# A state-space scan in a four-block transformer kernel: three per-chunk multiplies by C become one wide instruction, one state later

## The chip, the cores and the metric

The kernel runs on one core of a Trainium2 chip. The metric is the device time of one execution in microseconds (us), lower is better. It is the median of three executions.

## The reference, cut to what matters

The reference computes four sublayers on an input of 4 x 512 tokens of width 512, each followed by a residual addition and a layer norm: a selective state-space model (SSM), a mixture of experts, an attention, and a quantised MLP. The change touches the SSM alone. For one sequence `b`, one channel `d` of 512 and one state `n` of 16:

```
dt    = softplus(x_proj[:16] @ dt_proj + bias)          # per token and channel
dA    = exp(dt * A[d, n])
dBx   = dt * B[t, n] * x
h[t]  = dA[t] * h[t-1] + dBx[t]                         # the scan over 512 tokens
y[t]  = sum over n of C[t, n] * h[t, n]   + D * x
```

## The kernel before, in words

**Tiling.** Channels lie on the 128 partitions, so 512 channels make four chunks (`KC` = 4, c = 0 to 3), and the tokens of one sequence (`NB` = 512) lie along the free dimension. There are four sequences (`BATCH`, called batches below, b) of 16 states (`STATE`), so 64 steps n = 16 b + m, m being the state within the batch. Each step has four scans, one for each chunk.

**The engines' parts in one step**, all in `ssm` (L132 to L689). ScalarE (ACT) makes `da` = exp(dt A) for one chunk at a time into a ring of two PSUM tiles (L424); it may write the tile for scan i only when scan i - 2 is done (L417). GpSimd (POOL) makes `dbx` for all four chunks in one wide multiply (`inputs`, L294) into a ring of two. It may begin `dbx` of step n once the last scan of step n - 2 is done (L293). VectorE (DVE) runs the four scans (L561). TensorE (PE) spreads the row C[., n] over all partitions with one matmul into the one PSUM tile `cbc` (`spread`, L632), and may do so only when the multiplies of the step before have read it. DVE multiplies a chunk of `h` by `cbc` (`weigh`, L510), into a ring of two tiles `hc` of one chunk each. PE adds the product into the PSUM tile `y` of that chunk with a multiplication by the identity (`gather`, L651). The last chunk (c = 3) is multiplied by POOL instead (`weigh_last`, L305, from a copy of C in SBUF that a DMA broadcast; its gather is L646), except in the states m = 5 and 6 of batches 0 to 2, where DVE does it too (`pooled`, L188), because POOL has other work for the next batch close by.

**The order.** Each engine has its queue, written out by hand, and semaphores tie them. On DVE, `weigh(n, c-1)` stands right behind scan c of step n (L563), so that it never waits for the scan in front of it. At a batch's first state (m = 0) DVE also reads the finished sums of the batch before (`sums`, L523): chunks 0 to 2 behind scans 1 to 3 of m = 0, and chunk 3 at m = 2. At m = 2 of batches 0 and 1 it splits the C rows of a later batch into two parts (`split_c`, L459 and L461).

**Work for later batches**, spread over the states of a batch. ACT has the pieces of the softplus (L433 to L445): at count j = 4 m + c = 15 it takes a logarithm (L397), with a table load before and one behind it. At j = 36, 40, 48, 52 it copies a finished dt chunk (`copy_dt`, L401). PE projects rows (`project_rows`, L589) and dt (`project_z`, L605) for batch b + 2, and adds up the parts of dt for batch b + 1 in the states of `SUMMED` (L146), each time with four full fp32 matmuls (L615 to L621). POOL multiplies the masked logarithm (L271) twice in m = 7 and twice in m = 8, and dt by x (`scaled_x`, L276) in m = 11, 12, 13 and 15. There `inputs` of the next step stands behind it on POOL's queue.

After the last step, DVE reads the sums of batch 3 (L575), and a block boundary lets the layer norm begin.

## Time and profile before

| | us |
|---|---|
| median of the runs before | 1925.83 (1924.51 to 1928.50, 3 runs) |
| the profiled execution's own time, given as its span | 1927.0 |
| DVE busy over the span | 1494.8 (78%) |
| PE busy | 1704.9 (88%) |
| POOL busy | 688.5 (36%) |
| the 256 scans (DVE, L561) | 304.6 |
| the 198 multiplies by C on DVE (L510) | 131.3 |
| the 63 wide multiplies on POOL (L294) | 285.5 |

Only the span is known of the profiled execution, and it stands for its time. The table's shares are over the whole program. The SSM is its first part, from the start to about 464 us, and what matters there is read from that stretch alone. Busy time counts an instruction from its start to its end; where an engine's instructions overlap a little at their ends, the distance from one start to the next is what an instruction costs its queue.

### The profile page before, as it was taken

What the parts mean: (1) busy time and instruction counts of PE and PEld (TensorE: products, weight loads), DVE (VectorE), ACT (ScalarE), POOL (GpSimd) and SP (SyncE); (2) the same over time, 40 slices, a digit from 0 to 9 for tenths busy, and PEclk for the clock granted to TensorE, in tenths of its full rate; (3) what the DMA queues carried; (4) which work ended last, traced back from release to release, by engine and by line L of the source; (5) the groups of instructions that cost most, each with busy time, mean ns of one, the idle gap of its engine ahead of it and who ended that gap; (6) DMA issues with size and microseconds to landing.
All of it is one profiled execution on the core that took longest, in us unless ns stands there. A gap on an engine that the chain in (4) does not pass through costs nothing. (4 is left out here: it accounts for less than half of the span.)

```text
span 1927.0 us, 24366 instructions
## 1 busy us (share of the span) xinstructions
PE 1704.9 (88%) x7730; PEld 1038.8 (54%) x7730; DVE 1494.8 (78%) x2746; ACT 826.9 (43%) x1384; POOL 688.5 (36%) x419
## 2 busy tenths in 40 slices
PE   7888979777999995997788888888989999999997
PEld 2232323223677774885233333334768778788786
DVE  7999999999866666731788898884876776776677
ACT  5657464443414554321367777776521111111112
POOL 5898989996065544201130000000031320330100
PEclk8999989999999997998699999999989999999999
DMA  5344342331059996744443333320010000000002
GB/s 146 102 123 129 96 134 87 100 86 54 7 190 389 415 413 228 265 187 173 114 118 93 94 94 93 88 77 3 1 66 1 34 34 1 33 33 1 1 1 88
DMA packets 110702, 211.63 MB, mean 110 GB/s; under 512 B 18907, under 2 KB 35675, under 8 KB 109681
## 3 DMA queue, kind: packets, MB, share of 16 engines
q1 hardware_dynamic: 105457, 193.30, 30.5%
q0 software_dynamic: 5120, 16.78, 2.6%
q8 instruction: 64, 1.05, 0.2%
q14 instruction: 61, 0.50, 0.1%
HBM read 144.95 MB, written 62.65 MB: 108 GB/s over the span
## 5 line engine op out<-in xcount | busy, mean ns | idle before, releaser
L2022 DVE TENSOR_REDUCE att_top<-att_first 128x1 f32<-128x512 f32 x512 | 332.1, 686 | 70.3 <-PE att_first L1902 62.9
L561 DVE TENSOR_TENSOR_SCAN ssm_h<-ssm_da,ssm_dbx 128x512 f32<-128x512 f32 x256 | 304.6, 1207 | 6.4 <-ACT ssm_da L424 6.1
L294 POOL TENSOR_TENSOR ssm_dbx<-ssm_u,ssm_bbc 128x2048 f32<-128x2048 f32 x63 | 285.5, 4533 | 34.0 <-DVE ssm_h L561 30.8
L1984 ACT ACTIVATE att_prob<-att_second 128x1024 f32<-128x1024 f32 x256 | 248.1, 1022 | 87.5 <-PE att_second L1922 82.3
L651 PE MATMUL ssm_y<-ssm_hc,all_ident 128*128 128x512 f32 x396 | 224.3, 651 | 68.7 <-DVE ssm_hc L510 63.1
L424 ACT ACTIVATE ssm_da<-ssm_dt,ssm_minus_a 128x512 f32<-128x512 f32 x256 | 176.8, 691 | 188.7 <-DVE ssm_h L561 188.5
L2412 ACT ACTIVATE ffn_silu<-ffn_pg 128x256 f32<-128x256 f32 x112 | 43.2, 386 | 406.5 <-PE ffn_pg L129 406.5
L2277 POOL TENSOR_TENSOR pairs_raw<-pairs_raw,pairs_scales 128x512 f32<-128x512 f32 x42 | 42.3, 1042 | 489.7 <-DMA pairs_raw<-in_w 489.7
L1902 PE MATMUL att_first<-att_ks,att_qs 48*128 48x512 f32 x512 | 133.4, 510 | 65.2 <-DVE att_top L2022 50.5
L127 PE MATMUL ffn_pg<-pairs_wh,last_XH 128*128 128x512 f32 x448 | 176.7, 394 | 1.7 <-PEq L2080 1.7
L128 PE MATMUL ffn_pg<-pairs_wl,last_XH 128*128 128x512 f32 x448 | 176.5, 394 | 0.0
L129 PE MATMUL ffn_pg<-pairs_wh,last_XL 128*128 128x512 f32 x448 | 175.6, 392 | 0.0
L651 PEld LDWEIGHTS ssm_y<-ssm_hc,all_ident 128*128 128x128 f32 x396 | 65.1, 197 | 178.0 <-DVE ssm_hc L510 122.3
L1902 PEld LDWEIGHTS att_first<-att_ks,att_qs 48*128 48x128 f32 x512 | 53.6, 191 | 193.9 <-DVE att_top L2022 133.6
L2445 DVE TENSOR_TENSOR ffn_h<-ffn_pg,ffn_silu 128x256 f32<-128x256 f32 x112 | 47.4, 423 | 128.0 <-ACT ffn_silu L2412 127.7
L1937 PE MATMUL att_out<-att_prob,att_v 128*32 128x512 f32 x1024 | 137.2, 608 | 0.1
L510 DVE TENSOR_TENSOR ssm_hc<-ssm_cbc,ssm_h 128x512 f32<-128x512 f32 x198 | 131.3, 663 | 3.2 <-DVE ssm_h L561 2.1
L2284 POOL TENSOR_SCALAR pairs_wh<-pairs_raw 128x512 fp32r<-128x512 f32 x42 | 24.9, 628 | 234.3 <-PE ffn_py L129 234.3
L127 PE MATMUL ffn_py<-pairs_wh,ffn_hh 128*128 128x512 f32 x224 | 98.4, 439 | 0.0
L127 PEld LDWEIGHTS ffn_pg<-pairs_wh,last_XH 128*128 128x128 f32 x448 | 84.8, 189 | 21.8 <-issue 2.1
L1922 PE MATMUL att_second<-att_qs,att_ks 56*128 56x512 f32 x512 | 92.3, 416 | 4.7 <-DMA att_qs<-att_rows 2.9
L129 PEld LDWEIGHTS ffn_pg<-pairs_wh,last_XL 128*128 128x128 f32 x448 | 84.7, 189 | 18.7
(335 smaller groups left out, 3570.2 us busy)
## 6 DMA issues: line engine op xcount, KB each, us to landing
all_X<-in_w SPq DMA_DIRECT2D x29, 769.0 KB, 10.2
ssm_bbc<-brow_dram SPq DMA_DIRECT2D x64, 256.0 KB, 4.1
ssm_cbs<-crow_dram SPq DMA_DIRECT2D x58, 256.0 KB, 3.5
att_qs<-qk_dram SPq DMA_DIRECT2D x192, 64.0 KB, 2.2
att_ks<-qk_dram SPq DMA_DIRECT2D x192, 64.0 KB, 2.2
sorted_x<-ssm_zero SPq DMA_DIRECT2D x47, 256.0 KB, 3.6
sorted_y<-exp_y SPq DMA_DIRECT2D x47, 256.0 KB, 10.5
mlps_raw<-in_w SPq DMA_DIRECT2D x14, 769.0 KB, 9.8
```

The costliest lines, as they stand in the source:

```text
L127: pe.matmul(out, lh, rh, start=first, stop=False)
L128: pe.matmul(out, lh, rl, start=False, stop=False)
L129: return pe.matmul(out, ll, rh, start=False, stop=last)
L294: nc.gpsimd.tensor_tensor(dbx[:, n % 2], u[:, n // STATE % 2], bbc[:, n % RING, :].unsqueeze(1).to_broadcast([P, KC, NB]), ALU.mult).then_ ...
L424: nc.scalar.activation(da[:, i % 2, :], dt[:, b % 2, c, :], ACT.Exp, scale=minus_a[:, c, n % STATE:n % STATE + 1]).then_inc(da_ready, 1)
L510: nc.vector.tensor_tensor(hc[:, k % 2, :], cbc[:], h[:, n % 2, c, :], ALU.mult).then_inc(hc_ready, 1)
L561: nc.vector.tensor_tensor_scan(h[:, n % 2, c, :], da[:, i % 2, :], dbx[:, n % 2, c, :], 0.0, ALU.mult, ALU.add).then_inc(h_ready, 1)
L651: pe.matmul(y[:, c, :], g.ident[:], hc[:, k % 2, :], start=(m == 0), stop=(m == STATE - 1)).then_inc(y_own, 1)
L1902: pe.matmul(p_first[first_place(m) % FIRSTS][:], qs[w % RING][at, pair, qt * P:(qt + 1) * P], ks[w % RING][at, pair, :], start=True, stop= ...
L1937: mm = pe.matmul(p_out[VPAD * j:VPAD * (j + 1), :], v[s % RING][:, kt, VPAD * j:VPAD * (j + 1)], prob[step % 2][:, j, :], start=(kt == 0), ...
L1984: nc.scalar.activation(prob[step % 2][:, js, :], p_second[second_place(step, pair) % 2][:], ACT.Exp, scale=DK ** -0.5).then_inc(exp_done, 1)
L2022: nc.vector.tensor_reduce(top[w % 2][:, qt, item:item + 1], p_first[first_place(m) % FIRSTS][:], AX.X, ALU.max).then_inc(max_done, 1)
```

## The change

DVE's multiplies by C move one step later and become wide. For step n - 1 one instruction multiplies chunks 0 to 2 (0 to 3 in the states in which POOL does not take the last chunk) by `cbc`, read again for each chunk. It stands behind scan 1 of step n (behind scan 0 in the last step). `hc` becomes a ring of two steps of four chunks, and its semaphores count steps. The last step is still multiplied chunk by chunk, one behind scan 2, one behind scan 3 and one after the scans. PE's gathers of a step follow its wide multiply, so they come behind `spread` of the next step. The dt sums move to the states 6, 7, 9 and 10, the row projection to the front of m = 0, and the dt projection from m = 2..5 to m = 1..4. On DVE `sums` of chunks 0 to 2 move from m = 0 to m = 1, and the first waits for all of the batch's gathers of DVE's chunks. `split_c` moves from behind scan 1 to behind scan 2 of m = 2.

```diff
-        SUMMED = (7, 8, 10, 11)
+        SUMMED = (6, 7, 9, 10)
...
-        hc = sb("hc", [P, 2, NB])
+        hc = sb("hc", [P, 2, KC, NB])
...
-        def by_dve(n):
-            return KC * n - by_pool(n)
+        def wide(n):
+
+            return LAST if pooled(n) else KC
+
+        def weighed(n, c):
+
+            return n + 1 if n + 1 < STEPS else n + c + 1
...
-            def weigh(n, c):
-                k = by_dve(n) + c
-                dve.wait_ge(h_ready, KC * n + c + 1)
+            def weigh(n, lo, hi):
+                dve.wait_ge(h_ready, KC * n + hi)
                 dve.wait_ge(c_ready, n + 1)
-                if k >= 2:
-
-                    dve.wait_ge(y_own, k - 1)
-                nc.vector.tensor_tensor(hc[:, k % 2, :], cbc[:], h[:, n % 2, c, :], ALU.mult).then_inc(hc_ready, 1)
+                if n >= 2:
+
+                    dve.wait_ge(y_own, n - 1)
+                nc.vector.tensor_tensor(hc[:, n % 2, lo:hi, :], cbc[:].unsqueeze(1).to_broadcast([P, hi - lo, NB]),
+                                        h[:, n % 2, lo:hi, :], ALU.mult).then_inc(hc_ready, 1)
 
             def sums(b, c):
                 if c < LAST:
 
-                    dve.wait_ge(y_own, by_dve(STATE * (b + 1) - 1) + c + 1)
+                    dve.wait_ge(y_own, STATE * (b + 1))
...
                         if c < LAST or not pooled(n - 2):
-                            dve.wait_ge(hc_ready, by_dve(n - 2) + c + 1)
+                            dve.wait_ge(hc_ready, n - 1)
...
-                    if c:
-                        weigh(n, c - 1)
-                    elif n and not pooled(n - 1):
-                        weigh(n - 1, LAST)
                     if n == 0 and c == 0:
                         split_c(1)
-                    if m == 2 and c == 1 and b + 2 < BATCH:
+                    if b and m == 1 and c < 2:
+                        sums(b - 1, c)
+                        if c:
+                            sums(b - 1, c + 1)
+                    if n and c == (1 if n + 1 < STEPS else 0):
+                        weigh(n - 1, 0, wide(n - 1))
+                    if n + 1 == STEPS and c >= 2:
+                        weigh(n, c - 2, c - 1)
+                    if m == 2 and c == 2 and b + 2 < BATCH:
                         split_c(b + 2)
-                    if b and m == 0 and c:
-                        sums(b - 1, c - 1)
                     if b and m == 2 and c == 0:
                         sums(b - 1, LAST)
+            weigh(STEPS - 1, LAST - 1, LAST)
...
-                    pe.wait_ge(hc_ready, by_dve(n))
+                    pe.wait_ge(hc_ready, n)
...
-                    k = by_dve(n) + c
-                    pe.wait_ge(hc_ready, k + 1)
-                    pe.matmul(y[:, c, :], g.ident[:], hc[:, k % 2, :], start=(m == 0),
-                              stop=(m == STATE - 1)).then_inc(y_own, 1)
+                    pe.wait_ge(hc_ready, weighed(n, c))
+                    mm = pe.matmul(y[:, c, :], g.ident[:], hc[:, n % 2, c, :], start=(m == 0), stop=(m == STATE - 1))
+                    if c == wide(n) - 1:
+                        mm.then_inc(y_own, 1)
...
-                for c in range(LAST):
-                    if c == LAST - 1 and pooled(n) and n + 1 < STEPS:
-                        spread(n + 1)
+                if m == 0 and b + 2 < BATCH:
+                    for c in range(KC):
+                        project_rows(b + 2, c)
+                if n + 1 < STEPS:
+                    spread(n + 1)
+                for c in range(wide(n)):
                     gather(n, c)
-                    if n >= 2 and c == 0 and pooled(n - 2):
-                        gather(n - 2, LAST)
-                    if b + 2 < BATCH:
-                        if m == 0:
-                            project_rows(b + 2, c)
-                        if m == 1 and c == 0:
-                            project_rows(b + 2, LAST)
-                        if 2 <= m < 2 + KC and c == 1:
-                            project_z(b + 2, m - 2)
+                    if n and c == 0 and pooled(n - 1):
+                        gather(n - 1, LAST)
+                    if b + 2 < BATCH and 1 <= m < 1 + KC and c == 1:
+                        project_z(b + 2, m - 1)
                     if b + 1 < BATCH and m in SUMMED and c == LAST - 2:
                         sum_dt_first(b + 1, SUMMED.index(m))
                     if b + 1 < BATCH and m in SUMMED and c == LAST - 1:
                         sum_dt_last(b + 1, SUMMED.index(m))
-                if not pooled(n):
-                    if n + 1 < STEPS:
-                        spread(n + 1)
-                    gather(n, LAST)
-            gather(STEPS - 2, LAST)
             gather(STEPS - 1, LAST)
```

## Rows read from the trace of the kernel before

**Rows 1.** The first line of the profile's page.

```profile
span 1927.0 us, 24366 instructions
```

**Rows 2.** Windows, batch 1: busy of PE, PEld, DVE, ACT, POOL; clock, DMA, GB/s.

```profile
145.00:258.00 113.00, 96.68 (x197) 34.68 (x197) 109.92 (x126) 66.45 (x100) 102.52 (x41) 0.96 0.36 112
```

**Rows 3.** Groups by line, all scans (32 to 461 us): busy, mean ns, idle before.

```profile
L294 POOL TENSOR_TENSOR ssm_dbx<-ssm_u,ssm_bbc 128x2048 f32<-128x2048 f32 x63 | 285.5, 4533 | 34.0 <-DVE ssm_h L561 30.8 <-PE ssm_y L646 2.9
...
L510 DVE TENSOR_TENSOR ssm_hc<-ssm_cbc,ssm_h 128x512 f32<-128x512 f32 x198 | 131.3, 663 | 3.2 <-DVE ssm_h L561 2.1 <-PE ssm_cbc L632 0.4
```

**Rows 4.** DVE's waits, all scans: total, times, longest in us.

```profile
DVE ssm_h L561 <- ACT ssm_da L424: 6.1, 3, 2.1
DVE ssm_hc L510 <- DVE ssm_h L561: 2.1, 3, 0.7
```

**Rows 5.** Timeline (start, duration, engine, line) of DVE, one state of batch 3.

```profile
391.05 2.32 DVE L561 TENSOR_TENSOR_SCAN ssm_h<-ssm_da,ssm_dbx 128x512 f32<-128x512 f32 x2
393.30 0.66 DVE L510 TENSOR_TENSOR ssm_hc<-ssm_cbc,ssm_h 128x512 f32<-128x512 f32 x1
393.88 1.21 DVE L561 TENSOR_TENSOR_SCAN ssm_h<-ssm_da,ssm_dbx 128x512 f32<-128x512 f32 x1
...
397.30 2.32 DVE L561 TENSOR_TENSOR_SCAN ssm_h<-ssm_da,ssm_dbx 128x512 f32<-128x512 f32 x2
```

**Rows 6.** Groups by line and form: two-tensor operations of DVE, of two widths.

```profile
L1423 DVE TENSOR_TENSOR mlps_wl<-all_X,mlps_wh 128x1024 fp32r<-128x1024 f32 x29 | 35.2, 1215 | 0.0
...
L496 DVE TENSOR_TENSOR ssm_u<-ssm_dt,all_sums 128x512 f32<-128x512 f32 x4 | 2.5, 681 | 0.0
```

**Rows 7.** Timeline of POOL and DVE, the scans' first steps.

```profile
36.11 9.03 POOL L294 TENSOR_TENSOR ssm_dbx<-ssm_u,ssm_bbc 128x2048 f32<-128x2048 f32 x2
...
40.72 2.34 DVE L561 TENSOR_TENSOR_SCAN ssm_h<-ssm_da,ssm_dbx 128x512 f32<-128x512 f32 x2
```

**Rows 8.** Timeline of POOL, batch 0, from state 11's dbx to batch 1's first.

```profile
102.37 4.52 POOL L294 TENSOR_TENSOR ssm_dbx<-ssm_u,ssm_bbc 128x2048 f32<-128x2048 f32 x1 [0.85 <-DVE ssm_h L561]
106.85 1.27 POOL L305 TENSOR_TENSOR ssm_hp<-ssm_cbs,ssm_h 128x512 f32<-128x512 f32 x1
108.07 1.27 POOL L276 TENSOR_TENSOR ssm_u<-ssm_dt,all_sums 128x512 f32<-128x512 f32 x1
109.30 4.54 POOL L294 TENSOR_TENSOR ssm_dbx<-ssm_u,ssm_bbc 128x2048 f32<-128x2048 f32 x1
...
136.00 4.52 POOL L294 TENSOR_TENSOR ssm_dbx<-ssm_u,ssm_bbc 128x2048 f32<-128x2048 f32 x1
```

**Rows 9.** Timeline of DVE: state 12's wait, and batch 1's first scans.

```profile
118.09 0.69 DVE L510 TENSOR_TENSOR ssm_hc<-ssm_cbc,ssm_h 128x512 f32<-128x512 f32 x1 [0.70 <-DVE ssm_h L561]
...
141.13 2.32 DVE L561 TENSOR_TENSOR_SCAN ssm_h<-ssm_da,ssm_dbx 128x512 f32<-128x512 f32 x2
```

**Rows 10.** Timeline of PE: two gathers and a spread back to back.

```profile
121.46 1.02 PE L646 MATMUL ssm_y<-ssm_hp,all_ident 128*128 128x512 f32 x2
122.32 1.02 PE L651 MATMUL ssm_y<-ssm_hc,all_ident 128*128 128x512 f32 x2
123.27 0.49 PE L632 MATMUL ssm_cbc<-ssm_c_parts,ssm_sel 64*128 64x512 f32 x1
```

**Rows 11.** Timeline of ACT and DVE around the logarithm, batch 1, state 3.

```profile
166.53 0.68 ACT L424 ACTIVATE ssm_da<-ssm_dt,ssm_minus_a 128x512 f32<-128x512 f32 x1
...
172.47 2.35 DVE L561 TENSOR_TENSOR_SCAN ssm_h<-ssm_da,ssm_dbx 128x512 f32<-128x512 f32 x2 [2.05 <-ACT ssm_da L424]
```

**Rows 12.** Timeline of DVE: the last scan and the last sum.

```profile
458.11 1.21 DVE L561 TENSOR_TENSOR_SCAN ssm_h<-ssm_da,ssm_dbx 128x512 f32<-128x512 f32 x1
...
462.84 0.75 DVE L523 SCALAR_TENSOR_TENSOR all_sums<-all_sums,ssm_d,ssm_y 128x512 f32<-128x512 f32 x1 [0.96 <-PE ssm_y L646]
```

**Rows 13.** Windows: a stretch of batch 3 with a lower granted clock.

```profile
444.00:448.00 4.00, 3.97 (x6) 1.70 (x6) 4.00 (x5) 1.50 (x3) 3.50 (x3) 0.58 0.00 0
```

**Rows 14.** Timeline of PE: the gather that begins that stretch.

```profile
444.03 2.08 PE L651 MATMUL ssm_y<-ssm_hc,all_ident 128*128 128x512 f32 x2 [1.27 <-DVE ssm_hc L510]
```

## The prediction

> **What bounds the kernel now.** I read the page's first line for the profiled execution's length [rows 1]: 1927.0 us, 1.2 above the median of 1925.83. The sum is made against 1927.0, and the difference from the median is taken off at the end. The change lies within the scans, so the next views are of that stretch alone. The windows of batch 1 show DVE busy for 109.9 of 113 us and POOL for 102.5 [rows 2]: DVE bounds the stage, with POOL close behind. The groups by line name POOL's big item, 63 multiplies of 4.53 us with only 34 us of idle time before them in 428 us, and DVE's 198 multiplies by C of 0.663 us [rows 3]. DVE waits three times for ACT, 2.05 us each, at the logarithm, and three times 0.7 us in front of a multiply [rows 4]. The timeline gives the price that counts, the distance between starts [rows 5]: a state lasts 397.30 - 391.05 = 6.25 us. Two scans take 2.25, so a scan costs 1.125, and a multiply costs 393.88 - 393.30 = 0.58, although each lasts 0.66: the next instruction starts before this one has ended.
>
> **The wide multiply.** No row has its form. By width, a two-tensor operation takes 681 ns for 512 columns and 1215 for 1024 [rows 6], which is 1.043 ns a column. Three chunks then cost 0.58 + 1024 x 0.001043 = 1.65 us instead of 3 x 0.58 = 1.74, and four cost 2.18 instead of 2.32. Bounds: the multiplies' full fixed part would give 0.663 - 0.534 = 0.129 us for each instruction saved, not 0.58 - 0.534 = 0.046; at the other end reading C again for each chunk could cost as much as it saves, and the state stays at 6.25. I take 0.046, since rows 5 are this very queue. A state of DVE is then 4 x 1.125 + 1.65 = 6.15.
>
> The page "VectorE: DVE Perf Modes" of the Trainium skill (section on the TRN2 errata) gives a PSUM-source instruction a fixed cost of 120 cycles at 0.96 GHz, paid between instructions. By it each saved instruction would bring 0.125 us, and the sum would be the first rival's. The start-to-start distance in rows 5 disagrees.
>
> **The sum, by stretches.** Phases: "E" is the end of scan 3 of a batch's state 9, where POOL's chain of [rows 8] begins.
>
> 1. Up to the first scan of step 1 nothing changes: that scan starts at 40.72, just when POOL's first wide `dbx` is there (36.11 + 4.5 = 40.6) [rows 7]. The three multiplies of step 0 that lay in this wait leave it and have to be done later.
>
> 2. Batch 0, from there to E. Before, 28 multiplies: three for each of states 1 to 8, the extra ones of states 5 and 6, two of state 9: 16.24 us. After, the wide ones of states 0 to 8, 7 x 1.65 + 2 x 2.18 = 15.9. Gain 0.35, and 0.4 of a wait for PE in [rows 3] goes. At the logarithm ACT needs 172.47 - 166.53 = 5.94 us from its start behind scan 13 to scan 16 [rows 11], on either kernel. DVE covers it with 3 x 0.58 + 2 x 1.125 = 3.99 before and 1.65 + 2.25 = 3.90 after. Cost 0.1. Together -0.65.
>
> 3. Batches 1 and 2, first scan to E. 31 x 0.58 = 17.98 against 8 x 1.65 + 2 x 2.18 = 17.56: -0.4. The logarithm +0.1. New: `sums` of chunk 0 stands behind scan 0 of m = 1, and waits for all gathers of m = 15, which begin after the wide multiply of m = 15. PE needs 0.49 + 4 x 0.86 = 3.93 us for the spread and four gathers (the last chunk of m = 14 among them), the distances from [rows 10], and some 0.2 for the hand-over and the last result. DVE has three scans to fill it, 3.38. Wait 0.7, which holds up the scans behind it; POOL and ACT do not need it. +0.4 a batch, +0.8.
>
> 4. E to the next batch, three times. Before, 141.13 - 102.37 = 38.76 us [rows 8, 9]. POOL's own chain there has six `dbx` (4.48 apart), five multiplies of the last chunk (1.22) and four by x (1.23) without a stop, 136.00 + 4.52 - 102.37 = 38.15 long [rows 8], plus 0.08 to the scan. DVE's part shrinks to 6 x 6.15 - 0.2 = 36.7, since PE's dt sums, one state earlier, no longer hold up state 12 [rows 9]. So POOL ends the stretch and gives 38.23. Gain 0.53 each, -1.6, where DVE alone would have gained 2.1 each. The moved PE work: in states 6, 7, 9, 10 the dt sum adds 4 x 0.86 to 3.93, 7.4 us in a state of 6.15, but the next spread and the free half of `hc` are wanted only in the next state but one, some 11 us after the wide multiply. ACT's copy of the fourth dt chunk comes within 0.5 us of its sum, under POOL's bound. Row projection (3.4 us) ends before the next spread may start. SP's queue keeps its order and waits; each broadcast is issued four steps ahead. These I cost at nothing.
>
> 5. Batch 3 to the last scan's end: 47 x 0.58 = 27.26 against 16 x 1.65 + 0.58 = 26.98, and the wait of point 3. +0.4.
>
> 6. The tail. Before, the last scan ends at 459.32 and the last sum at 463.59, 4.27 later [rows 12]. After, PE has from the end of step 62's wide multiply a spread and four gathers (3.93) and then four more (3.44) to do before the first three sums may begin, which is about 7.55 after that multiply with the hand-overs. The last scan ends 2.25 + 0.58 + 1.21 = 4.04 after it, so they begin 3.5 behind it; three sums (0.75 long each [rows 12], some 0.65 apart) and a fourth end 6.2 behind. +1.95. It is on the path: a block boundary follows.
>
> Sum: -0.65 + 0.8 - 1.6 + 0.4 + 1.95 = +0.9, so 1927.9 for the profiled execution, and 1926.7 for the median. **The forecast is no change**: about 4 us of DVE time are saved and 3.5 us of PE's waits go, and POOL's chain, the late sums and the tail take them.
>
> **The rivals.**
>
> *Each saved instruction is worth its whole fixed part* (faster). Outside POOL's stretches DVE issues 19 + 21 + 21 + 30 = 91 fewer multiplies. At 0.083 more each that is -7.5: about 1919. For it: the 0.66 duration. Against it: 0.58 between starts, for all of the multiplies that do not wait. Chance 0.07.
>
> *POOL and PE give way* (faster). If POOL's chain runs in the shadow (-4.6, for example because DVE's long read of PSUM leaves it freer) or the sums and the tail wait less than worked out (up to -4), the result is 1919 to 1923. Against it: POOL's durations hardly vary. Chance 0.2.
>
> *The granted clock falls at the batch ends* (slower). Before, PE's gathers are spread over the state, its longest idle time being 1 to 2 us; after, they come in one run with 2.2 us of idle in front. In batch 3 the granted clock was 0.58 in one stretch of 4 us (1.2 GHz for most of it) [rows 13], and a gather took 2.08 us instead of 1.12 [rows 14]; two gathers so slowed cost PE 1.7 us. In mid-batch the 7 us of slack hide that. It decides where DVE waits for PE: at three batch ends and the tail, from the first microsecond, since these waits exist already. 4 x 1.7 = 6.8 more: 1933.5. Chance 0.18.
>
> *The wide form gains nothing* (reading C thrice costs what it saves, the edit does not do what it says): 45 wide multiplies outside POOL's stretches at 0.09 to 0.14 more, +4 to +6: 1931. Chance 0.05.
>
> **How the numbers follow.** The forecast has 0.5, its own range 1923 to 1930 (the hand-overs and ACT's short slack, each some tenths, four times). The range of 1919 to 1933 takes in the faster rivals and most of the slow one, and leaves out a tenth on either side. Two tenths of a per cent, 3.9 us, is about what a measurement of this kernel tells from no change. Below 1922.0: 0.07, most of the second rival, a little of the forecast, together 0.26. Above 1929.7: the clock, the last rival, and some of the forecast, 0.26. Between: 0.48.
>
> **What would show it.** Right: L510 with 63 wide instructions of about 1.73 us (2.27 for four chunks) and three of 0.66; a state of 6.15 in batch 3; POOL without idle from state 11 to the next batch, and DVE's scans waiting for L294 at states 14 and 16; a DVE wait of 0.7 for PE in front of L523 at m = 1, three times; about 6.2 us from the last scan's end to the last sum's; no wait at state 12. Wrong: wide multiplies under 1.65 us or starts less than 1.6 apart, a POOL chain with gaps, waits for PE of over 2 us in front of L523 with a clock near 0.5.

## The result, and the profile after

The changed kernel takes 1940.95 us (median of 6 executions, 1938.44 to 1945.41) against 1928.95 (1924.51 to 1931.46, 6 executions) for the kernel before, measured beside it. The ratio is 1.0058, with a 95% interval of 1.0042 to 1.0074: slower by 0.6%, some 12 us, and outside the forecast's range. The page's first line of the changed kernel [rows 1]:

```profile
span 1936.7 us, 24102 instructions
```

It grew by 9.7 us; the execution that was profiled is the lowest of the six. The difference sits in the scans: the last sum of the SSM ended at 463.59 us before and ends at 475.92 now, 12.3 later. (Behind it the program took 1463.4 us before and 1460.8 in this one execution; nothing there was changed, and the runs below have 1463.5 to 1468.2 on the chips where before was near 1930. I did not look into this. On the chip where before took 1954.52 it is 1487.5 to 1491.3, while the scans are as long there as on the others: a batch 3 without waits takes 101.30 on that chip and 101.31 elsewhere. So the scans are compared across chips below, and whole times only on one chip.)

The scans were cut into the prediction's stretches by the starts of DVE's scans in both traces (E is the end of a batch's state 9). This table is worked out from those starts:

| us | before | after | difference | forecast |
|---|---|---|---|---|
| start, to step 1 | 40.72 | 40.08 | -0.6 | 0 |
| batch 0, to E | 61.15 | 64.94 | +3.8 | -0.65 |
| E to batch 1 | 39.26 | 38.95 | -0.3 | -0.53 |
| batch 1, to E | 69.57 | 75.93 | +6.4 | +0.4 |
| E to batch 2 | 39.26 | 38.39 | -0.9 | -0.53 |
| batch 2, to E | 67.93 | 69.10 | +1.2 | +0.4 |
| E to batch 3 | 39.27 | 38.44 | -0.8 | -0.53 |
| batch 3 | 102.16 | 103.67 | +1.5 | +0.4 |
| last scan's end to last sum's | 4.26 | 6.41 | +2.15 | +1.95 |

So the two batches whose states also carry the dt projection, 0 and 1, lose 10 us between their first scan and E. In batch 1's windows (columns as in [rows 2]) DVE is no longer full: 102.94 us of 113, from 109.92, and PE's granted clock is 0.91, from 0.96:

```profile
145.00:258.00 113.00, 96.52 (x192) 36.98 (x191) 102.94 (x86) 62.14 (x96) 97.69 (x38) 0.91 0.33 108
```

The groups by line and form, DVE then POOL, over all scans (columns as in [rows 3]), have the wide multiply at 1.73 us for three chunks and 2.26 for four, no wait in front of it, and 21.7 us of idle time in front of the scans. L566 is the scan, L528 the sums, L514 the multiply by C, L299 POOL's `dbx`:

```profile
L566 DVE TENSOR_TENSOR_SCAN ssm_h<-ssm_da,ssm_dbx 128x512 f32<-128x512 f32 x256 | 294.5, 1202 | 21.7 <-ACT ssm_da L429 19.6 <-issue 2.0
L514 DVE TENSOR_TENSOR ssm_hc<-ssm_cbc,ssm_h 128x1536 f32<-128x1536 f32 x57 | 98.6, 1730 | 0.0
L514 DVE TENSOR_TENSOR ssm_hc<-ssm_cbc,ssm_h 128x2048 f32<-128x2048 f32 x6 | 13.6, 2263 | 0.0
...
L299 POOL TENSOR_TENSOR ssm_dbx<-ssm_u,ssm_bbc 128x2048 f32<-128x2048 f32 x63 | 285.6, 4534 | 45.0 <-DVE ssm_h L566 44.5
```

POOL's multiply is as long as before (4.53), and has 11 us more idle time: it follows a slower DVE. The waits (total, times, longest; compare [rows 4], where DVE waited 6.1 us for `da`) name two new ones:

```profile
DVE ssm_h L566 <- ACT ssm_da L429: 19.6, 12, 4.0
...
ACT all_X L354 <- PE ssm_aux L613: 13.7, 6, 4.4
...
DVE all_sums L528 <- PE ssm_y L658: 7.0, 4, 2.6
```

The waits of ACT for `ssm_aux` are where to begin. `all_X L354` is ACT's first piece of the softplus for a later batch (`magnitude`, at counts j = 13, 17, 21 and 25), and it reads PE's dt projection (`project_z`, L613). Before, ACT lost 2.5 us in six such waits, at most 0.4 at a time:

```profile
ACT all_X L349 <- PE ssm_aux L605: 2.5, 6, 0.4
```

One case in full, the third chunk in batch 1. Before, PE's timeline (start, duration) has two gathers and the projection, and ACT's magnitude follows it:

```profile
175.45 1.12 PE L651 MATMUL ssm_y<-ssm_hc,all_ident 128*128 128x512 f32 x2 [1.34 <-DVE ssm_hc L510]
176.42 1.02 PE L646 MATMUL ssm_y<-ssm_hp,all_ident 128*128 128x512 f32 x2
177.27 1.02 PE L651 MATMUL ssm_y<-ssm_hc,all_ident 128*128 128x512 f32 x2
178.23 1.12 PE L605 MATMUL ssm_aux<-ssm_rows,ssm_wdt 16*128 16x512 f32 x2
```

After, PE's timeline in the same place (L640 is the spread, L658 and L654 the gathers):

```profile
183.32 0.79 PE L640 MATMUL ssm_cbc<-ssm_c_parts,ssm_sel 64*128 64x512 f32 x1 [4.65 <-DVE ssm_hc L514]
184.04 2.08 PE L658 MATMUL ssm_y<-ssm_hc,all_ident 128*128 128x512 f32 x2
185.91 1.91 PE L654 MATMUL ssm_y<-ssm_hp,all_ident 128*128 128x512 f32 x2
187.61 1.91 PE L658 MATMUL ssm_y<-ssm_hc,all_ident 128*128 128x512 f32 x2
189.46 1.12 PE L613 MATMUL ssm_aux<-ssm_rows,ssm_wdt 16*128 16x512 f32 x2
```

The projection now stands behind everything that the one wide multiply releases, and the burst starts after 4.65 us of idle time with gathers twice as long. The window has the reason:

```profile
183.00:188.00 5.00, 4.68 (x6) 2.13 (x7) 5.00 (x6) 2.10 (x4) 2.35 (x1) 0.50 0.30 107
```

The granted clock is 0.50, which is 1.2 GHz throughout. The timelines of ACT and DVE show who pays:

```profile
190.62 0.69 ACT L354 ACTIVATE all_X<-ssm_aux,ssm_dtb 128x512 f32<-128x512 f32 x1 [4.37 <-PE ssm_aux L613]
191.20 0.68 ACT L429 ACTIVATE ssm_da<-ssm_dt,ssm_minus_a 128x512 f32<-128x512 f32 x1
```

```profile
179.26 2.35 DVE L566 TENSOR_TENSOR_SCAN ssm_h<-ssm_da,ssm_dbx 128x512 f32<-128x512 f32 x2 [3.78 <-ACT ssm_da L429]
181.53 1.73 DVE L514 TENSOR_TENSOR ssm_hc<-ssm_cbc,ssm_h 128x1536 f32<-128x1536 f32 x1
183.18 4.56 DVE L566 TENSOR_TENSOR_SCAN ssm_h<-ssm_da,ssm_dbx 128x512 f32<-128x512 f32 x4
187.65 1.73 DVE L514 TENSOR_TENSOR ssm_hc<-ssm_cbc,ssm_h 128x1536 f32<-128x1536 f32 x1
191.92 1.22 DVE L566 TENSOR_TENSOR_SCAN ssm_h<-ssm_da,ssm_dbx 128x512 f32<-128x512 f32 x1 [2.54 <-ACT ssm_da L429]
```

ACT stands 4.37 us at the magnitude, and the `da` queued behind it, which does not need the projection, comes 2.54 us too late for the scan. How much room there was can be read here. Without the wait the scan would start at 189.38. It starts 191.92 - 190.62 = 1.30 after the magnitude does. So the projection has to end by 188.08, which is 4.82 behind the end of the wide multiply (181.53 + 1.73). It ended 7.32 behind. Both traces together have sixteen cases of that distance (a batch's four chunks, batches 0 and 1). Before, it is 2.23 us in six, and 3.9 in the two at state 3, where PE's clock was low (0.72 and 0.77) and ACT had its logarithm to do and did not wait. After, it is 4.37 in the one case at a full clock with nothing late ahead of it. It is 6.0 to 7.3 in four whose burst ran at 1.2 GHz for part or all of it, and 4.9, 5.5 and 6.5 in three at a full clock that stood behind such a burst.

The wait of 3.78 at 179.26 is the logarithm's (2.05 before, [rows 11]); the magnitude that stands just ahead of it on ACT had waited 1.46 for its projection. In batch 0 the magnitude there waited 2.80, and the logarithm's wait is 4.00.

### The profile page after: what moved, and what is told of

Read it like the earlier page. It is cut to its first block and busy times, and to the rows that moved or that the text cites. A ratio compares the mean times of both kernels' runs of the same rounds, so it can differ in the third digit from the quotient of the medians.

```text
span 1936.7 us, 24102 instructions
## 1 busy us (share of the span) xinstructions
PE 1708.9 (88%) x7730; PEld 1051.5 (54%) x7730; DVE 1485.8 (77%) x2614; ACT 823.8 (43%) x1384; POOL 686.8 (35%) x419
## 5 line engine op out<-in xcount | busy, mean ns | idle before, releaser
L566 DVE TENSOR_TENSOR_SCAN ssm_h<-ssm_da,ssm_dbx 128x512 f32<-128x512 f32 x256 | 294.5, 1202 | 21.7 <-ACT ssm_da L429 19.6
L299 POOL TENSOR_TENSOR ssm_dbx<-ssm_u,ssm_bbc 128x2048 f32<-128x2048 f32 x63 | 285.6, 4534 | 45.0 <-DVE ssm_h L566 44.5
L658 PE MATMUL ssm_y<-ssm_hc,all_ident 128*128 128x512 f32 x396 | 218.4, 658 | 0.0
L658 PEld LDWEIGHTS ssm_y<-ssm_hc,all_ident 128*128 128x128 f32 x396 | 75.3, 205 | 93.3 <-issue 91.2
L514 DVE TENSOR_TENSOR ssm_hc<-ssm_cbc,ssm_h 128x1536 f32<-128x1536 f32 (+2 forms) x66 | 114.1, 1730 | 0.0
L640 PE MATMUL ssm_cbc<-ssm_c_parts,ssm_sel 64*128 64x512 f32 x64 | 34.4, 537 | 85.6 <-DVE ssm_hc L514 84.9
```

The lines of the kernel that those rows point to most:

```text
L299: nc.gpsimd.tensor_tensor(dbx[:, n % 2], u[:, n // STATE % 2], bbc[:, n % RING, :].unsqueeze(1).to_broadcast([P, KC, NB]), ALU.mult).then_ ...
L514: nc.vector.tensor_tensor(hc[:, n % 2, lo:hi, :], cbc[:].unsqueeze(1).to_broadcast([P, hi - lo, NB]), h[:, n % 2, lo:hi, :], ALU.mult).the ...
L566: nc.vector.tensor_tensor_scan(h[:, n % 2, c, :], da[:, i % 2, :], dbx[:, n % 2, c, :], 0.0, ALU.mult, ALU.add).then_inc(h_ready, 1)
L658: mm = pe.matmul(y[:, c, :], g.ident[:], hc[:, n % 2, c, :], start=(m == 0), stop=(m == STATE - 1))
```

## Two theories

**A, the order.** The loss of batches 0 and 1 comes from ACT standing in its queue for a projection that now lies behind the wide multiply, a spread and three gathers. Whatever takes ACT's wait away gives the loss back, at any clock. **B, the clock.** The order alone costs little; PE's granted clock falls after the longer idle times. Keep the clock up and the loss goes, with the order as it is. The rest (sums, tail, width, the moved dt sums) is a theory for each, tested by undoing that part.

All diffs are against the changed kernel unless said otherwise. "Last sum" is the end of the last sum of the SSM (463.59 before, 475.92 after).

## Experiments

**ACT's pieces one state later.** The projection stays late; ACT asks for it later.

```diff
-                    if j in (13, 17, 21, 25):
-                        magnitude(b + 2, (j - 13) // 4)
-                    if j in (14, 18, 22, 26):
-                        positive(b + 2, (j - 14) // 4)
+                    if j in (17, 21, 25, 29):
+                        magnitude(b + 2, (j - 17) // 4)
+                    if j in (18, 22, 26, 30):
+                        positive(b + 2, (j - 18) // 4)
```

> The changed kernel, with ACT's magnitude and positive pieces of the dt projection four counts (one state) later. Theory A (PE's projection comes too late behind the wide multiply, ACT blocks at the magnitude and the next da behind it is late): ACT's waits for aux at the magnitude fall from 13.7 us to under 2, DVE's waits for da from 19.6 to about 10.5 (1.6 at the start, 2.1 at each of three logarithms, 2.7 at the dt copies), batches 0 and 1 shorter by 3 and 5 us, span 8 to 9 below the changed kernel's 1936.7. Rival B (ACT's own load in a run of four scans on a ring of two da tiles makes da late): the same number of pieces in the same kind of place, DVE's waits for da stay near 19.6 and the span near 1936.7.

Measured: 1937.19 us (9 executions) against 1929.85 for before, ratio 1.0043 (1.0024 to 1.0062). The last sum ends at 467.15, 8.8 earlier than in the changed kernel. Batch 0 takes 60.08 (from 64.94) and batch 1 69.86 (from 75.93), and ACT's wait for the projection is gone. The span fell by 5.1 (1931.6), not by the 8 to 9 expected, because behind the SSM this execution took 1464.4 and that of the changed kernel 1460.8. DVE's waits:

```profile
DVE ssm_h L566 <- ACT ssm_da L429: 7.0, 5, 2.1
DVE all_sums L528 <- PE ssm_y L658: 7.0, 4, 2.6
```

DVE's wait for `da` falls from 19.6 to 7.0, the three logarithms that were there before (6.1). Not all of the 10.9 us that batches 0 and 1 got back passes through this queue position: in batch 1 the first sum waited 0.93 instead of 2.60, a wait for PE's gathers and not for ACT, and this is 1.67. Of the other 9.3, 9.1 lie in states 3 and 5 of the two batches, in which DVE had waited for `da`. Batch 3 took 1.6 us more this time (105.30), with one sum that waited 2.6, which is part of why the last sum shows 8.8. The medians say less than the traces (1937.2 against 1940.9): single executions of this kernel lie between 1931 and 1944, and the intervals of the two ratios overlap, so the whole times alone do not show the gain.

**Zero products in PE's idle time.** The kernel adds one or two products with a tile of zeros into `y` ahead of each spread, so that PE idles less; no value changes.

```diff
+                if m:
+                    for _ in range((1 if 1 <= m <= 4 and b < 2 else 2) if m not in (6, 7, 8, 9, 10, 11, 12) or b == BATCH - 1 else 0):
+                        pe.matmul(y[:, 0, :], g.ident[:], zero[:], start=False, stop=False)
                 if n + 1 < STEPS:
                     spread(n + 1)
```

> The changed kernel, with PE adding one or two products of a zero tile into y's chunk 0 in its idle time (two a state, one in states 1 to 4 of batches 0 and 1, none in states 6 to 12 of batches 0 to 2), which leaves the values as they are. Theory A1 (PE is late because its granted clock is at 1.2 GHz after the long idle time in front of each run of gathers): the granted clock in the scans rises from about 0.85 to over 0.97, ACT's waits for aux fall from 13.7 to under 5, DVE's for the sums from 7.0 to about 3, span 7 to 10 below 1936.7. Rival A2 (PE is late by its order alone, four gathers and the spread ahead of the projection at either clock): the clock rises, the waits change by less than a third, span within 3 us of 1936.7.

Measured: 1937.03 (8 executions), ratio 1.0036 (1.002 to 1.0052). Batch 1 takes 71.47 (from 75.93) with a granted clock of 0.98, batch 0 63.77 (from 64.94) with 0.91. The products reached into the tail, which grew from 6.41 to 8.91. In batch 0 the clock still fell. The window there, and the same case on ACT:

```profile
65.00:70.00 5.00, 3.04 (x4) 1.46 (x5) 5.00 (x5) 3.75 (x7) 1.66 (x2) 0.68 0.56 170
```

```profile
74.49 0.69 ACT L354 ACTIVATE all_X<-ssm_aux,ssm_dtb 128x512 f32<-128x512 f32 x1 [4.60 <-PE ssm_aux L613]
```

So the clock is part of it, but this kernel doesn't say how much: the products also delay PE, and where they held the clock up and where they did not lie in different batches.

**More products at the logarithm.** DVE waits longest at state 3's logarithm, and PE with it, so five products went there (this kernel and the later one have none in the tail). The diff is against the kernel just shown.

```diff
-(1 if 1 <= m <= 4 and b < 2 else 2)
+((1, 1, 1, 5)[m - 1] if 1 <= m <= 4 and b < 2 else 2)
```

> As the filler run before, but with five zero products at the top of state 4 of batches 0 and 1, where PE stood idle for 2.9 us behind the logarithm and the granted clock fell to 1.2 GHz (and none in the last three steps). Clock theory: the granted clock is full through states 3 to 5 of batch 0, ACT's wait for aux at the magnitude of state 5 falls from 4.6 to about 2 us, the period of state 5 from 9.05 to under 6.6, batch 0 to about 61.5 and batch 1 to about 70. Rival (order alone: the projection stands behind the wide multiply, the spread and three gathers): the wait stays above 3.5 us and state 5 above 8 us.

Measured: one execution of 1967.34, on a chip on which before took 1954.52. The clock fell again at the logarithm of batch 0 (0.84 in 65 to 70 us, 0.82 in 70 to 75), and batch 0 took 65.63. The five stood behind state 3's gathers, not ahead of them: PE ran them after the idle time that they were meant to fill. It doesn't decide between A and B as I had meant it to, but it shows that lateness costs without the clock. The five put off the next burst, the projection of the fourth chunk ended 9.49 us behind its multiply at a granted clock of 1.00, ACT waited 5.16 for it, DVE 2.76, and state 6 became 9.6 us long. One iteration earlier they are in the idle time itself:

```diff
-((1, 1, 1, 5)[m - 1] if 1 <= m <= 4 and b < 2 else 2)
+((1, 1, 5, 1)[m - 1] if 1 <= m <= 4 and b < 2 else 2)
```

> The filler run again with its mistake mended: the five zero products stand at the top of step 3 (PE's idle time behind the logarithm lies in front of the spread and gathers of state 3), one in states 1, 2 and 4. Clock theory: the granted clock stays at 1 from 55 to 80 us, the projection of the third chunk ends 4.4 us behind its wide multiply instead of 6.0 to 6.3, ACT waits about 2 us for it instead of 3.1 to 4.6, and DVE's scans of state 5 wait under 0.5 us instead of 1.2 to 2.8; states 5 of batches 0 and 1 last under 6.8 us. Rival (order alone): DVE still waits over 1.2 us there.

Measured: one execution of 1939.76, before 1930.65. Batch 0 takes 61.10 and its state 5 6.99, a little above the 6.8 that I had put as the clock theory's limit. The windows over the same place, then the case on ACT and on DVE:

```profile
65.00:75.00 10.00, 10.00 (x23) 3.72 (x21) 9.30 (x8) 6.32 (x12) 7.28 (x4) 1.00 0.27 85
```

```profile
72.96 0.69 ACT L354 ACTIVATE all_X<-ssm_aux,ssm_dtb 128x512 f32<-128x512 f32 x1 [2.53 <-PE ssm_aux L613]
```

```profile
74.26 2.41 DVE L566 TENSOR_TENSOR_SCAN ssm_h<-ssm_da,ssm_dbx 128x512 f32<-128x512 f32 x2 [0.70 <-ACT ssm_da L429]
```

At a full clock ACT still waits 2.53 us, but only 0.70 of it reaches DVE, and the projection is 1.1 us later than the order alone makes it, by the last of the five products. Without that the projection ends 4.37 behind the multiply, inside the 4.82 worked out above. So in this state the order alone takes nearly all the slack and costs little, and the clock's 1.6 to 2.9 us on top are what DVE pays. In batch 1 the clock fell in the burst with the first chunk's projection (0.72), and DVE waited 3.9 at the logarithm behind it.

The same case, the third chunk, can be lined up over the seven kernels that leave the projection behind the burst and ACT's pieces early (the changed one, the three with zero products, and three further down: narrow multiplies, dt sums in their old states, and sums and tail mended). In three of its fourteen cases the distance is 4.38 and DVE does not wait. In the other eleven it is 5.5 to 7.6, and DVE waits the distance less 4.78, within 0.01 in ten and 0.12 in one. (The room of 4.82 above is the same, counted to ACT's start, 0.04 behind the projection's end.) For the first chunk the wait goes into the logarithm's, which was 2.05 before: 2.1 to 2.2 at a distance of 4.37, 3.88 at 6.08, and 4.00 with 0.95 more ahead of it at 7.31. **So neither theory holds alone.** The new order at a full clock costs DVE at most 0.2 us a batch, which is B's part. But it leaves only 0.4 of the 4.8 us of room, and then everything that makes PE late, a burst at 1.2 GHz or products put in its way, comes through to DVE. In the old order a distance of 3.9 at a low clock cost nothing.

**The projection in PE's idle time.** Here the chunks 2 and 3 are projected at the head of the iteration, ahead of the spread, while PE waits for DVE anyway. ACT's pieces stay where the change left them. The sums and the tail are mended too, as in the next but one below, and the diff shows the projection's part alone.

```diff
+                if b + 2 < BATCH and 3 <= m < 1 + KC:
+                    project_z(b + 2, m - 1)
                 if n + 1 < STEPS:
                     spread(n + 1)
...
-                    if b + 2 < BATCH and 1 <= m < 1 + KC and c == 1:
+                    if b + 2 < BATCH and 1 <= m < 3 and c == 1:
                         project_z(b + 2, m - 1)
```

> The changed kernel with the sums and the tail moved as before, ACT's pieces where the changed kernel has them, and PE's projection of chunks 2 and 3 at the top of steps 3 and 4, ahead of the spread, in the time in which PE waits for the wide multiply. If the projection's place behind the wide multiply is what costs, at either clock: ACT's waits for aux fall from 10.3 (the run without this edit) to under 3, states 5 last 6.2 instead of 7.5 and 8.9, batch 0 is 60.1 to 60.5 and batch 1 about 69.5, the last sum ends near 460, and the ratio to the kernel before is 0.997. Rival (PE, late at 1.2 GHz, reaches the top of the step late as well): ACT's waits stay above 6 and states 5 above 7.2.

Measured: 1925.75 (12 executions) against 1930.65 (23), ratio 0.9983 (0.9971 to 0.9994): faster than before, by 0.2%. Batch 0 takes 60.22, batch 1 69.31, and the last sum ends at 460.00; the same kernel with the projection left behind the burst (three below) has 61.60, 72.15 and 462.18. Its waits (total, times, longest):

```profile
DVE ssm_h L566 <- ACT ssm_da L429: 9.2, 7, 2.2
...
ACT all_X L354 <- PE ssm_aux L613: 1.0, 2, 0.5
```

PE's timeline has the projection done before the burst, and it has the burst at both speeds, the second after 2.53 us of idle time. DVE feels neither:

```profile
180.37 1.09 PE L613 MATMUL ssm_aux<-ssm_rows,ssm_wdt 16*128 16x512 f32 x2
181.63 0.50 PE L640 MATMUL ssm_cbc<-ssm_c_parts,ssm_sel 64*128 64x512 f32 x1 [0.17 <-DVE ssm_hc L514]
182.06 1.12 PE L658 MATMUL ssm_y<-ssm_hc,all_ident 128*128 128x512 f32 x2
...
188.28 0.53 PE L640 MATMUL ssm_cbc<-ssm_c_parts,ssm_sel 64*128 64x512 f32 x1 [2.53 <-DVE ssm_hc L514]
188.74 2.08 PE L658 MATMUL ssm_y<-ssm_hc,all_ident 128*128 128x512 f32 x2
```

In batch 0 the burst right behind the moved projection of the third chunk was a slow one too (granted clock 0.76 from 66 to 72 us), and DVE's scans did not wait behind it. In these kernels a slow burst cost only where another engine's queue stood behind it.

**The sums behind the multiply.** ACT's pieces late, and in m = 1 of DVE's order the wide multiply first, with one sum after each of scans 1 to 3.

```diff
-                    if b and m == 1 and c < 2:
-                        sums(b - 1, c)
-                        if c:
-                            sums(b - 1, c + 1)
                     if n and c == (1 if n + 1 < STEPS else 0):
                         weigh(n - 1, 0, wide(n - 1))
+                    if b and m == 1 and c:
+                        sums(b - 1, c - 1)
```

> The changed kernel with ACT's magnitude pieces one state later and DVE's sums of chunks 0 to 2 behind the wide multiply of state 1 and scans 1 to 3 instead of in front of it. If the sums wait because PE cannot have finished the gathers of state 15 by then: DVE's waits for y at the sums vanish but for the tail's 2.5, state 1 of batches 1 to 3 falls from 9.13 to about 8.1 and state 2 from 8.1 to about 6.9 (8.4 with split), each batch boundary 2 us shorter: span 6 below the magnitude run's 1931.6, near 1926. Rival (the wait moves to PE, which must wait for the sums before it may start y again, and comes back in the last chunk's sum at state 2): state 2 stays above 7.8.

Measured: one execution of 1949.76, before 1954.52 on that chip. Batches 1, 2 and 3 take 68.83, 67.24 and 101.30, each 1.0 to 4.0 less than with ACT's pieces late alone (69.86, 69.62, 105.30), the last sum ends at 460.56, and of the waits in front of sums only the tail's is left:

```profile
DVE all_sums L528 <- PE ssm_y L656: 2.5, 1, 2.5
```

**The tail as well.** Step 62's multiply stands right behind its own scan 3, step 63's gathers count singly, and each last sum waits for its own gather.

```diff
-                    dve.wait_ge(y_own, STATE * (b + 1))
+                    dve.wait_ge(y_own, STATE * (b + 1) + (c if b == BATCH - 1 else 0))
...
-                    if n and c == (1 if n + 1 < STEPS else 0):
+                    if n and c == 1 and n + 1 < STEPS:
                         weigh(n - 1, 0, wide(n - 1))
+                    if n + 2 == STEPS and c == LAST:
+                        weigh(n, 0, wide(n))
...
-                    if c == wide(n) - 1:
+                    if c == wide(n) - 1 or n + 1 == STEPS:
                         mm.then_inc(y_own, 1)
```

> As the run with magnitude and sums moved, and in the last two steps the wide multiply of step 62 stands behind its own scan 3, and the last sums wait for their own chunk alone. Tail: from the last scan's end to the last sum's end 6.4 falls to about 4.5, span about 1924, 2 to 3 below the kernel before, ratio to it 0.998 to 0.999. Rival (PE's nine products bound the tail wherever the sums stand): tail above 6.

Measured: 1948.73 (12 executions) against 1954.52 (17), ratio 0.9972 (0.996 to 0.9985). The last sum ends 4.35 us behind the last scan (6.41 in the changed kernel, 4.26 before), the four sums in one piece, with no wait in front of the first:

```profile
457.07 3.25 DVE L528 SCALAR_TENSOR_TENSOR all_sums<-all_sums,ssm_d,ssm_y 128x512 f32<-128x512 f32 x4
```

**The same with ACT's pieces back early.** This is the kernel just shown, with `magnitude` at 13, 17, 21, 25 again.

> As the run before but with the magnitude pieces where the changed kernel has them, so that it parts their share: if they cost what the first run showed, batch 0 is 64 to 65 and batch 1 over 73 long again, and the span 9 to 11 above the run with all three. Rival (the boundary waits had caused the late projection): batch 1 within 1 us of the run with all three.

Measured: one execution of 1955.16, before 1954.52. Batch 0 takes 61.60 and batch 1 72.15, against 60.07 and 69.23 with the pieces late: 4.4 us for the place of the pieces, where in the unmended kernel it was 9.3 (10.9 less the sum's 1.67). I had expected the span 9 to 11 longer, and it is 4.9. ACT waits for the projection as before (10.3 us in six). What differs is where PE's clock is low when a projection is due; I read that from the traces, and no run sets it. So the mechanism holds and its size doesn't: it goes, as far as the traces tell, with where in the batch PE's clock falls.

**Narrow multiplies in the new place.** This keeps the new order and takes only the width away.

```diff
-                nc.vector.tensor_tensor(hc[:, n % 2, lo:hi, :], cbc[:].unsqueeze(1).to_broadcast([P, hi - lo, NB]),
-                                        h[:, n % 2, lo:hi, :], ALU.mult).then_inc(hc_ready, 1)
+                for c in range(lo, hi):
+                    one = nc.vector.tensor_tensor(hc[:, n % 2, c, :], cbc[:], h[:, n % 2, c, :], ALU.mult)
+                    if c == hi - 1:
+                        one.then_inc(hc_ready, 1)
```

> The changed kernel, with the wide multiply issued as three (or four) narrow ones in the same place, the last one signalling. It parts the width from the place. If the width is worth 0.05 us for each instruction saved, a state of batch 3 is 6.24 to 6.25 instead of 6.12, and batch 3 is 2 us longer than the changed kernel's; POOL's stretches (state 10 to the next batch) stay within 0.3. The place alone then costs the whole loss: the span is 2 to 4 above 1936.7. Rival (the wide form itself harms, by holding cbc or h longer): the span falls below 1936.7.

Measured: one execution of 1947.83. In steady states of batch 3 a state is 6.25 us long, as before; with the wide form it is 403.70 to 409.83, 6.13, by DVE's timeline of the changed kernel:

```profile
403.70 1.73 DVE L514 TENSOR_TENSOR ssm_hc<-ssm_cbc,ssm_h 128x1536 f32<-128x1536 f32 x1
405.35 4.55 DVE L566 TENSOR_TENSOR_SCAN ssm_h<-ssm_da,ssm_dbx 128x512 f32<-128x512 f32 x4
409.83 1.73 DVE L514 TENSOR_TENSOR ssm_hc<-ssm_cbc,ssm_h 128x1536 f32<-128x1536 f32 x1
```

The last sum ends at 481.83, 5.9 later, and the span is 9.4 longer, where I had expected 2 to 4. Part of that is not the width: of batch 3's 108.95 us, 4.17 are a wait in front of a sum, with a low clock on PE. A cleaner comparison is the mended kernel with narrow multiplies (ACT's pieces, sums and tail as above):

> The fastest run so far (magnitude, sums and tail moved) with narrow multiplies in place of the wide ones. The width's share with the waits gone: 0.13 a state where DVE bounds (45 states of 64), 5 to 6 us, so the last sum ends at 465 to 466, later than the kernel before's 463.6, and the ratio to before is 1.000 to 1.002: what the best version gains comes from the width alone. Rival (the gain comes from the dt sums' move and the new places, not the width): the last sum ends before 462.

Measured: 1932.93 (10 executions) against 1930.65, ratio 1.0012 (0.9999 to 1.0025). The last sum ends at 465.27, against 460.32 for the same kernel with wide multiplies. DVE's timeline has the period of before, 408.06 - 401.80 = 6.26:

```profile
401.80 4.56 DVE L568 TENSOR_TENSOR_SCAN ssm_h<-ssm_da,ssm_dbx 128x512 f32<-128x512 f32 x4
406.28 1.86 DVE L515 TENSOR_TENSOR ssm_hc<-ssm_cbc,ssm_h 128x512 f32<-128x512 f32 x3
408.06 2.33 DVE L568 TENSOR_TENSOR_SCAN ssm_h<-ssm_da,ssm_dbx 128x512 f32<-128x512 f32 x2
```

So what is gained in the mended kernels is the width's 5 us, and the new order by itself brings nothing (+1.7 at the last sum against the kernel before, and no clear difference in the whole time). Between E and the next batch this narrow kernel takes 38.4 to 38.7, like the wide ones: there POOL's chain sets the length, not the multiplies.

**The dt sums in their old states.**

```diff
-        SUMMED = (6, 7, 9, 10)
+        SUMMED = (7, 8, 10, 11)
```

> The changed kernel with the dt sums back in states 7, 8, 10 and 11. If the move by one state was needed (ACT's copy of dt chunk 0 stands at state 9, and the sums of a state now run in the state after it): DVE's waits for da grow by 2 to 4 us in each of batches 0 to 2, the span by 5 to 10. Rival (the move brought nothing, since POOL's chain ends these stretches): the stretch from state 10 to the next batch stays within 0.5 of 38.4 and the span within 2 of 1936.7.

Measured: one execution of 2010.53. The stretches from E to the next batch take 57.94, 57.40 and 58.85 us instead of 38.4 to 39.0. I had expected 2 to 4 more in each, and it was 19 to 20. The waits:

```profile
DVE ssm_h L566 <- ACT ssm_da L429: 88.2, 16, 8.7
ACT ssm_dt L406 <- PE ssm_aux L629: 80.7, 12, 9.0
```

ACT's copy of a dt chunk stands 9 us for its sum, and `da` for all scans stands behind it: the same queue, the same fault, six times as large. The move of the dt sums is a needed part of this change.

## Why the prediction was wrong

**The step that failed** is point 4, "The moved PE work". It counted what PE's extra work does to PE's own next spread, and to ACT's copy of the fourth dt chunk, then said of all of it "These I cost at nothing". The dt projection was left out altogether: that it moves from behind two gathers of a narrow multiply to behind a spread and three gathers of a wide one, and that ACT's `magnitude` and the `da` behind it wait for it. Its place is in points 2 and 3, batches 0 and 1. The trace of the kernel before could have sized it: the distance goes from 2.23 us to 0.49 + 3 x 0.86 + 1.1 = 4.2 at a full clock [rows 10], and with three gathers 0.96 longer each [rows 14] to 7.1. Measured were 4.37 and up to 7.32, against the 4.8 of room, so up to 2.5 past it. Moving ACT's pieces alone returned 4.86 us in batch 0 and 4.4 in batch 1 (6.07 less the sum's 1.67), where 3.8 and 6.4 had been lost against the kernel before.

**The third rival, the clock,** had the mechanism, and the wrong place for most of it. The granted clock did fall after longer idle times (0.96 to 0.91 in batch 1). The rival said "In mid-batch the 7 us of slack hide that". Those 7 us are the slack of the next spread, not of the projection, which had about 0.5 left. At the batch ends, where it put the cost, the first sum waited 2.60 at one of three, with a granted clock of 0.81 around it, and 0.93 and 0.92 at the other two: the 1.7 that the rival asked for was paid once, and not at all in the tail (2.51 at a full clock). The page "TensorE: Matmul & The Clock Gate" of the Trainium skill (section "HAM oscillation — how this bites in real kernels") says that a matmul burst that ends in a wait each time can begin cold (at the lower clock) each time. The trace agrees: the burst behind 4.65 us of idle time ran with a granted clock of 0.50.

Point by point:
- *The wide multiply*: 1.73 long, as given. A state is 6.12 to 6.13, forecast 6.15: 0.065 us saved for each instruction that goes, where 0.046 was taken. From start to start the wide multiply takes 1.65 (403.70 to 405.35), just as forecast, and its four scans 4.48 instead of 4.50. The first rival's 0.129, and the 0.125 of the page "VectorE: DVE Perf Modes" of the Trainium skill (section on the TRN2 errata), would give 5.99 to 6.00, and no state shows that. Over the scans the width is worth 5 us, which also settles the last rival (the wide form gains nothing).
- *Point 1*: nothing forecast, -0.6 measured. Starts of the same point in the runs differ by a microsecond (39.83 to 41.15), so it is no effect to explain.
- *Point 2*: -0.65 forecast, +3.8 measured. With ACT's pieces late it is -1.1, so the step without the projection was about right.
- *Point 3*: the wait of `sums` was forecast at 0.7 each time. It was 2.60, 0.93 and 0.92 in the three batches. The sum of the last chunk at m = 2 waited too in two of them, 0.71 and 1.23, which was not forecast: its gather now lies one burst later. Batches 2 and 3 are +1.2 and +1.5 instead of +0.4 each.
- *Point 4, POOL's bound*: -0.3, -0.9, -0.8 for three times -0.53, and POOL's durations unchanged. Right, and the narrow kernel has it too.
- *Point 6, the tail*: 6.41 for 6.2, and mending it gives 4.35. Right.

In sum the forecast had +0.9, and the last sum moved +12.3. Of the 11.4 between them, about 10 are batches 0 and 1, and 1.9 batches 2 and 3.

**What stays open.** What a late projection costs is known case by case. What a whole kernel loses by it varies with where PE's clock is low, from 4.4 us in one pair of kernels to 9.3 in the other, and no run sets that. No run has the new order with a full clock in both batches either: it was held up in batch 0 alone. Whether products of other data than zeros hold the clock up differently was not tried. The two mended kernels ran on different chips, so which of them is better isn't known (their last sums end at 460.32 and 460.00), nor were the earlier projection and the later pieces joined.

## What to carry to other kernels

When work moves on one engine, list each result that it delays and go to the instruction that reads it, on every other engine. An in-order queue that stands for a result which nobody needs yet (softplus for a batch two ahead) also holds back the work behind it that is needed now, so compare its new arrival with the time at which the queue gets there, not with when the value is used. Where many small releases become one large one, put the pieces that others wait for ahead of the burst, in the idle time that the merging made, and price the burst at both levels of TensorE's clock.

## What was not expected of the hardware

Merging made PE's work no longer but its idle times longer (from about 1.3 us at these places to 2.7 to 5.4 in four of the eight cases), and with them came the lower clock: PE is busy as long as before in batch 1's window (96.68 and 96.52 us), in which the SSM now gets less far. Overlap on DVE is larger than busy times suggest: two instructions merged into their neighbour save 0.065 us each, a tenth of the 0.66 that each is busy. And the dt sums' place showed how steep such a queue is: one state later on PE, 19 us more in each batch.
